# A hint for the loop's closing branch at the head of two of the kernel's loops, on four engines

## The reference

```
x = _layernorm(x + _L0_attn_ref(x, ...))       # min_gru scan, 16-head causal attention, gated FFN
x = _layernorm(x + _L0_xattn_ref(x, ctx, ...)) # 16-head cross attention
x = _layernorm(x + _L0_ffn_ref(x, ...))        # FFN quantised with one scale over ALL of x
x = _layernorm(x + _L1_attn_ref(x, ...))       # gated delta rule: short conv, chunked state, 16 heads
x = _layernorm(x + _L1_xattn_ref(x, ctx, ...)) # cross attention
x = _layernorm(x + _L1_ffn_ref(x, ...))        # squared ReLU FFN, then a count of five spikes
```

## Time and profile before

| | us |
|---|---|
| median of the 3 timed runs | 3034.99 |
| lowest and highest of them | 3032.06, 3039.45 |
| the profiled execution | 3039.48 |
| its span, first to last instruction | 3037.7 |

### The profile page before, as it was taken

One profiled execution on the slowest core, in us unless ns is written; L12 is line 12 of the kernel. 1 busy time (PEld: TensorE's weight loads), 2 busy tenths in 40 slices (PEclk: granted clock), 3 DMA queues, 4 the chain that ended last, 5 costly groups with the idle time before them and its releaser, 6 DMA issues.

```text
span 3037.7 us, 101152 instructions
## 1 busy us (share of the span) xinstructions
PE 2646.6 (87%) x41928; PEld 1912.2 (63%) x41928; DVE 1673.0 (55%) x3917; ACT 1641.1 (54%) x3841; POOL 304.2 (10%) x270
## 2 busy tenths in 40 slices
PE   3888888888888847989889889899899898898897
PEld 2656555656556625676667667666676676666665
DVE  3556566566566564545545545555455455465454
ACT  2556556556556514556555555555555555555563
POOL 0000000000000000110110110111111011101101
PEclk9999999999999977999999999999999999999999
DMA  3000000000000010000000000000000000000000
GB/s 95 6 7 5 7 6 5 5 6 5 8 5 5 5 43 6 8 6 6 8 6 6 8 6 6 8 6 7 8 6 7 6 8 6 7 5 8 6 6 4
DMA packets 50578, 28.41 MB, mean 9 GB/s; under 512 B 19792, under 2 KB 48528, under 8 KB 50256
## 3 DMA queue, kind: packets, MB, share of 16 engines
q1 hardware_dynamic: 50256, 23.25, 2.7%
HBM read 17.98 MB, written 5.24 MB: 8 GB/s over the span
## 4 chain that ended last, share of the span: by engine, by line
PE 47%; ACT 5%; issue 5%; DVE 4%; POOL 1%; POOLq 0%; DMA 0%; ACTq 0%; SPq 0%; DVEq 0%
PE bank L359 6%; PE bank L1093 4%; PE bank L1223 3%; PE bank L1160 2%; PE bank L1123 2%; PE bank L1290 2%; PE bank L1133 2%; PE bank L1209 2%; PE bank L394 2%; PE bank L1016 2%; PE bank L1207 2%; PE bank L1013 1%; PE bank L1258 1%; PE bank L377 1%; ACT zels L1341 1%
## 5 line engine op out<-in xcount | busy, mean ns | idle before, releaser
L359 PE MATMUL bank<-w_gate,ident 128*128 128x128 f32 (+3 forms) x1984 | 599.4, 390 | 0.0
L359 PEld LDWEIGHTS bank<-w_gate,ident 128*128 128x128 f32 x1984 | 310.8, 193 | 75.6 <-issue 56.2
L464 POOL TENSOR_TENSOR Kbd<-kT,headmask 128x512 f32<-128x512 f32 x96 | 99.7, 1039 | 2001.4 <-DVE kT L442 2001.4
L447 DVE TENSOR_REDUCE m<-bank 128x4 f32<-128x512 f32 x384 | 262.0, 682 | 44.4 <-PE bank L384 24.1
L394 PE MATMUL bank<-ident,zels 128*128 128x128 f32 x1536 | 230.4, 282 | 55.6 <-ACT zels L425 54.1
L449 DVE TENSOR_TENSOR zels<-bank,m 128x512 f32<-128x512 f32 x384 | 265.6, 692 | 13.2
L425 ACT ACTIVATE zels<-zels 128x512 f32<-128x512 f32 x384 | 231.9, 627 | 73.1 <-DVE zels L449 70.8
L1001 POOL TENSOR_TENSOR PT<-zels,unit 128x512 f32<-128x512 f32 x160 | 202.4, 1270 | 641.3 <-ACT zels L1341 501.2
L394 PEld LDWEIGHTS bank<-ident,zels 128*128 128x128 f32 x1536 | 173.4, 143 | 92.2 <-ACT zels L425 75.7
L428 ACT ACTIVATE PT<-bank 128x512 f32<-128x512 f32 x384 | 204.2, 594 | 16.3 <-PE bank L394 14.8
L1341 ACT ACTIVATE zels<-bank 128x512 f32<-128x512 f32 (+1 forms) x256 | 142.4, 572 | 107.4 <-PE bank L1192 58.8
(11 more groups left out here) (283 smaller groups left out, 5114.7 us busy)
## 6 DMA issues: line engine op xcount, KB each, us to landing
ctxT<-in_ctxT_dram SPq DMA_DIRECT2D x64, 48.0 KB, 1.8
x<-in_xT_dram SPq DMA_DIRECT2D x32, 64.0 KB
x_after_cross_attention<-x SPq DMA_DIRECT2D x32, 64.0 KB, 1.6
h<-x_after_cross_attention SPq DMA_DIRECT2D x8, 256.0 KB, 2.8
xin<-x_after_cross_attention SPq DMA_DIRECT2D x32, 64.0 KB, 1.8
out_dram<-xn SPq DMA_DIRECT2D x32, 64.0 KB, 1.6
input_integers<-xq SPq DMA_DIRECT2D x8, 128.0 KB, 2.0
xq<-input_integers SPq DMA_DIRECT2D x32, 32.0 KB, 1.8
```

The source lines that it names most:

```text
L359: mm(bank[:, 0:cols], ident[:, :], w_gate[:, :, :].rearrange("p a b -> p (a b)")[:, 0:cols], start=True, stop=True)
L447: dve.tensor_reduce(top, scores, AX_X, ALU.max).then_inc(ph.dve[s], ph.DV.step(s, f"{t}max{u}"))
```

## The change

`in_rounds` opens its loop with another call, which has the same bounds and the same single engine, and asks for a hint on the back edge. The call puts one branch-hint instruction at the very head of the body, ahead of the first slot, tied to the COMPARE_BRANCH at the body's end, and marks that branch as likely taken. The hint is executed on every round. Order, waits, operands and numbers of all other instructions are as before.

```diff
-    with eng.Fori(1, ROUNDS) as it:
+    with eng.bass.Fori(1, ROUNDS, engines=bass.OrderedEngineSet([eng.engine]), hint_back_edge=True) as it:
         before = eng.snap(it - 1)
         for s, stage, back in slots:
             advance(s, before if back else it, stage)
```

## The result

| | before | after |
|---|---|---|
| median of 5 runs | 3034.99 us (3032.06 to 3045.3) | 3015.13 us (3011.93 to 3018.23) |
| ratio, 95% interval | | 0.9917 [0.9901, 0.9932] |
| profiled execution: span, granted clock | 3037.7 us, 0.971 | 3013.3 us, 0.979 |

The change made the kernel 0.8% faster by the ratio of the single runs, and 0.7% by the two medians (3015.13 / 3034.99 = 0.9935). 2959 was forecast, with a range of 2943 to 3012, so the time lies just outside it. Of the 76 us that were to be gained, 20 (medians) to 24 (profiled executions) came.

A forecast was written before the change was run, and what follows sets the result against it. PE, busy 87% of the span, was taken to set the time. Savings of 80.8 - 4.0 - 0.9 = 75.9 us off the profiled 3039.48 gave 2963.6, so a median of 2959 us, range 2943 to 3012.

The forecast's parts named there:

- Where the stall is, and that the hint cures it: PE's third-stage closing branch: late fetch of the loop's head, 49.5 us in 14 gaps; hinted branch near 215 ns.
- does nothing: Rival: PE's third-stage branch stalls as before despite the hint; time about 3036 us, chance 0.11.
- fetches what is there: Rival: hints refetch resident loop heads, so loops that wrap quickly stall too; time about 3115 us, chance 0.07.
- A hinted round: PE's third-stage loop: 110.96 us a round, built on round 1, against 116.73; 80.8 us saved over 14 rounds.
- Other drops of the clock: Third-stage half-clock stretches before the branch, three in 14 rounds, expected to stay: 4.0 us given back, bounds 0 to 19.
- Leaving the loop: Late fetch of the code behind a hinted loop: taken as 0, bounds 0 to 7 us, 3.5 per stage.
- The hint itself: Hint instruction at the body's head: 0.06 us each; 0.9 us for PE's first stage, third-stage share counted in the round.
- Half a cure: Rival: third-stage fetch starts earlier but isn't finished, or the clock still drops; 3002 or 2989 us, chance 0.12.

The follow-up runs named there:

- e6: Changed kernel with the hint taken off PE's third-stage loop alone, the other seven hints kept: 3044.77 us, ratio 1.002 to the kernel before.
- e1: Kernel before, no hint, two semaphore increments ahead of PE's third stage to shift its code as the hints do: 3063.59 us, ratio 1.0092.
- e5: Changed kernel with PE's third-stage body back at its earlier place (one keep-warm matmul left out, two semaphore increments added): 2988.63 us, ratio 0.9834.
- e7: Changed kernel with PE's third-stage body begun 64 instructions into a code packet: 2964.32 us, ratio 0.9747 to the kernel before.
- e8: Changed kernel with PE's third-stage body begun 96 instructions into a code packet: 2967.98 us, ratio 0.9765 to the kernel before.
- e11: Kernel before, no hint, with 20 semaphore increments of PE directly behind its third-stage loop: 3042.68 us, ratio 1.0016.
- e2: Changed kernel with the hint on PE's third-stage loop alone, the seven others removed: 2991.28 us, ratio 0.9837 to the kernel before.
- e12: Changed kernel with the hint on PE's third-stage loop alone, its body begun 64 instructions into a code packet: 2961.01 us, ratio 0.975.

## Why the prediction was wrong, step by step

In the profiled executions 75.9 us were to go, and 24.4 went: 51.5 missing.

- **Where the stall is, and that the hint cures it: right.** The branch takes 458 ns at the median, no gap before line 1101 is over 0.51 us, and 18 code packets come a round (252 in 14) with the head's ahead of the branch. ACT, DVE, POOL and PE's first stage are as before but for hints of 31 to 39 ns and some 5 ns more a branch (ACT 49 for 45, DVE 61 for 56, POOL 49 for 45). The rivals "does nothing" and "fetches what is there" are out: between 240 and 1085 us one packet of code is fetched in after, and the seven hints of e6 come with first-stage branches and rounds as before (216 ns on PE, 64.77 us for 64.74). The Trainium skill's page "Runtime: NRT & Kernel Launch", section "Instruction fetch mechanics", says that prefetch is purely sequential. The runs with a hint contradict it: in after the head's packet is fetched 3.1 us ahead of the taken branch.
- **"A hinted round", 110.96: this is the step that failed**, with 114.23 measured, 3.27 in each of 14 rounds, 46 us, against which stand the 4.0 of the next step. It took round 1 as what any round is without the stall, "the same 2171 matmuls". The matmuls are the same; where they lie in the packets isn't. The prediction counted the hint's time and not its length. Two instructions moved a packet's end in front of the signal at line 1223. e1 shows this alone to cost 28 us, and e5 that it is 1.75 of the 3.27 us (114.23 - 112.48), the half-clock stretches behind the gap included. Of the other 1.5 the second packet of the body takes 0.8 (10.7 / 14 in e5; the gap at line 1223, 3 us behind the branch): it is asked for only behind the branch. The branch takes 0.44 in place of 0.22. Some 0.5 us a round is not accounted for. In e7, where neither packet's end hurts much, a round takes 110.96. The number was right for a place that the change didn't have, and that e7 gets there also by losing a gap that round 1 had is luck in part.
- **"Other drops of the clock", 4.0 given back: a small term with a wrong reason.** "Nothing of the stall is near", it said of the half-clock stretch at 1461.70. The 1.93 us of idle time that end 0.6 us before it are for the most part a late packet of code under ACT's name, and the two other stretches of before stand as close behind the same gap (0.2 and 0.9 us). In after there are eight in place of three, which at the forecast's own 1.35 us each is 11 us and not 4.0. e5, which has the gap of before without the stall, has two of them, and e7 and e8, which don't have the gap, none: these drops could have gone too. The 1.35 itself is not worked out in the prediction, and no run isolates it.
- **"Leaving the loop", 0 taken: wrong, 8.9 us.** The bound of 3.5 for a late fetch nearly held for the gap (3.65), but it left out the clock behind it, which e11 shows to be the larger part. The reason given for 0, that the head's packet need not displace the next one, failed: behind the last branch the next packet comes only 1.7 us later (in before it had come 3.4 ahead). The prediction had priced a stall at more than its length inside the loop, and didn't do so here.
- **The hint itself, 0.06: right** (36 ns on PE; twelve rounds of the first stage grew by 0.04 us each).
- **What the view of the earlier trace rows had shown and the prediction left out.** It holds 11.1 us of gaps at line 1233 that nothing ends (shown above), 15 of them, one a round and also in round 1, where no branch is near. They were the sign that a round has stalls of code inside. The same section of the Trainium skill says that crossing a block's border is mostly hidden; in the dense 64 x 64 stretches here a crossing costs 0.5 to 2.2 us.

Summed up: rounds 41.8 short (the forecast of 76.8 for them, after the 4.0, against 35.0), exit 8.9, round 1 1.4, and 0.6 the other way in what lies ahead of the loop, 51.5 in all. Half a cure, the second rival, came near in time (3002) and not in mechanism.

## What to carry to other kernels

Where an engine's loop body doesn't fit its instruction store, a hinted back edge is worth its stall and the clock behind it, but only with the place chosen as well: keep the last packet's end far enough ahead of the branch (3.7 us of work was enough here, 3.2 was not), and keep packet ends out of dense runs of small matmuls, above all off the instruction that carries a signal. Any edit that adds or takes away an instruction ahead of such a body moves all its packet ends: time the shift alone before giving an edit the credit or the blame. And look for stalls of code under other names: a gap that an engine is said to end which was done before, at the same instruction in every round, moves when the code is shifted.

## What the runs showed of the hardware

- Where PE waited for a packet of code inside a round, its next matmul came 2.2 to 2.9 us after the fetch. In after the gaps at 67 and 103 us of a round stand 1279 instruction records apart, which is five packets of 256 but for one record; 32 matmuls of 64 x 64 with their weight loads, 64 instructions, pass in some 0.6 us, a packet of them in 2.4.
- With a hint, the head's packet takes the place of the packet that follows the branch in the order of the code, which before the change was fetched in vain once a round, 2.8 to 3.5 us ahead of the branch: 18 packets in place of 19.
- A semaphore increment on PE has 51 ns in the trace at line 1142, but a row of 20 or 60 of them takes 0.155 us each (9.3 / 60, 3.14 / 20).
- One instruction fewer ahead of PE's body was worth 24 us (after 3015.13, e2 2991.28; e2 also lacks seven hints, and e12 against e7, at one place, shows those to be worth nothing that can be told: 2961.01 and 2964.32).
